# Gated attention and a top-2 expert layer: token rows scattered to expert slots in DRAM, in one engine block

## Time and profile before

| | |
|---|---|
| median of 3 runs | 1044.95 us (1043.86 to 1045.88) |
| profiled execution | 1039.82 us, its span 1038.1 us |
| busy share of the span | PE 96%, PE weight loads 82%, DVE 66%, ACT 46%, POOL 46% |
| mean granted TensorE clock | 0.988 |
| DMA | 63.42 MB, of which SP's queue 45.41 MB and POOL's queue 17.47 MB |

### The profile page before, as it was taken

One profiled execution on the slowest core, in us unless ns is written; L12 is line 12 of the kernel. 1 busy time (PEld: TensorE's weight loads), 2 busy tenths in 40 slices (PEclk: granted clock), 3 DMA queues, 4 the chain that ended last, 5 costly groups with the idle time before them and its releaser, 6 DMA issues. The chain is left out here.

```text
span 1038.1 us, 21103 instructions
## 1 busy us (share of the span) xinstructions
PE 993.9 (96%) x7314; PEld 855.4 (82%) x7314; DVE 682.9 (66%) x1607; ACT 477.9 (46%) x1502; POOL 482.6 (46%) x498
## 2 busy tenths in 40 slices
PE   6999999999999999999999997999999999999995
PEld 5778878878878778878878786799999899999995
DVE  5886895885885885885886866444455555444552
ACT  3664553553553553653553541344353544435351
POOL 7521071071071170270270153385858567585856
PEclk9999999999999999999999998999999999999998
DMA  9201110120020020021002001425345262523525
GB/s 247 84 9 54 42 48 13 40 61 7 34 61 20 20 61 33 8 61 56 4 0 61 3 1 41 133 37 132 61 107 127 62 147 35 132 56 102 122 55 66
DMA packets 49948, 63.42 MB, mean 61 GB/s; under 512 B 5976, under 2 KB 41714, under 8 KB 49906
## 3 DMA queue, kind: packets, MB, share of 16 engines
q1 hardware_dynamic: 37234, 45.41, 14.0%
q0 software_dynamic: 12672, 17.47, 10.0%
HBM read 46.45 MB, written 16.78 MB: 61 GB/s over the span
## 5 line engine op out<-in xcount | busy, mean ns | idle before, releaser
L1252 ACT ACTIVATE hid<-up,b 128x512 f32<-128x512 f32 x128 | 88.0, 687 | 86.2 <-PE up L1203 86.2
L722 ACT ACTIVATE work<-score,negmax 128x128 f32<-128x128 f32 x256 | 90.2, 379 | 80.6 <-DVE negmax L919 80.6
L1131 POOL DMA_INDIRECT out_dram<-eo,index_e x64 | 106.4, 1663 | 19.5 <-issue 18.9
L722 ACT ACTIVATE probs_odd<-score,negmax 128x128 f32<-128x128 f32 x256 | 90.2, 380 | 51.6 <-DVE negmax L919 51.6
L343 POOL TENSOR_SCALAR var<-mv 128x4 f32<-128x4 f32 (+1 forms) x17 | 3.8, 226 | 219.8 <-DVE mv L774 212.3
L1304 DVE TENSOR_TENSOR eo_raw<-down,b 128x256 f32<-128x256 f32 x64 | 25.9, 425 | 121.1 <-PE down L1217 121.1
L1297 DVE TENSOR_TENSOR hid_l<-hid,hid_h 128x512 fp32r<-128x512 f32 x128 | 88.7, 693 | 4.4
L675 ACT ACTIVATE q_sb<-proj 128x512 f32<-128x512 f32 x64 | 38.7, 604 | 108.9 <-PE proj L593 108.9
L1295 DVE CAST hid_h<-hid 128x512 fp32r<-128x512 f32 x128 | 54.7, 427 | 47.9 <-ACT hid L1252 46.2
L1260 ACT ACTIVATE eo<-eo_raw,gate_e 128x256 f32<-128x256 f32 x64 | 30.9, 506 | 118.1 <-DVE eo_raw L1304 118.1
L919 DVE TENSOR_REDUCE negmax<-score 128x4 f32<-128x512 f32 x128 | 81.9, 681 | 2.1 <-PE score L514 2.1
(11 more groups left out here) (217 smaller groups left out, 3067.2 us busy)
## 6 DMA issues: line engine op xcount, KB each, us to landing
w_raw<-fc1T_dram SPq DMA_DIRECT2D x9, 1024.0 KB, 5.3
w_raw<-fc_dram SPq DMA_DIRECT2D x9, 1024.0 KB, 9.3
rows<-x_dram SPq DMA_DIRECT2D x16, 512.0 KB, 4.6
out_dram<-rows SPq DMA_DIRECT2D x8, 512.0 KB, 3.0
xn_rows<-rows SPq DMA_DIRECT2D x8, 512.0 KB, 2.9
c_raw<-ctxT_dram SPq DMA_DIRECT2D x8, 256.0 KB, 3.9
c_raw<-ctxT_dram SPq DMA_DIRECT2D x16, 128.0 KB, 4.5
b<-fc2b_dram SPq DMA_DIRECT2D x9, 128.0 KB, 8.4
```

Source lines behind the costliest of these rows:

```text
L722: last = nc.scalar.activation(probs[j % 2][:, c, :], score[hh][:, b * P:(b + 1) * P], ACT.Exp, bias=negmax[:, j % 2, c:c + 1], accum_out=s ...
L1131: pool.indirect_dma_start(out=out_rows[:, :], out_offset=bass.IndirectOffsetOnAxis(ap=index_e[par][:, half * GB + i:half * GB + i + 1], ax ...
L1252: nc.scalar.activation(hid[m % 2][:, :], up[m % 2][:, :], ACT.Relu, bias=b1[par][:, m:m + 1]).then_inc(s_hid, 1)
```

## The change

1. Each group's rows are scattered to their slots. A tensor `disp` in DRAM has 8 x 1024 rows of 258 numbers: 256 features, the token number, and the exponential of the difference of the two best logits. A row stands in `packed` in SBUF; POOL issues eight indirect DMAs per group (two choices, four sequences), in `dispatch`, in the place where the one-hots were formed, so ahead of `copy_ck`. One-hots, T0/T1, the tables and their sums are gone, and so is the store of rows by SP. The second choices' real rank is compared with the capacity at once (`loc[:, 2]`).
2. `disp` is filled first by one SP DMA (zeros, and token number 4096, which is out of bounds), after the first two groups' loads.
3. Experts load their rows with plain SP DMAs, one per half, in place of gathers. DVE takes the token numbers and gate weights out of the last two columns (`meta`), at the start of each half.
4. Both parts stand in one block, and the block boundary is gone. In the hand-over the low parts of the first expert's weights go from POOL to DVE, one before the projection, one behind the slots; ACT's second high part moves behind the exponential; the warm-up matmuls of 3, 6 and 24 become one run of 40, and those of 26 ahead of the first transposes go.
5. The first two jobs of a group wait for the read-out of FA/FB (`s_f_split`) instead of the table sums.

The diff, cut to its core:

```diff
-MISC_PREV = {1: ["O0", "O1"], 2: ["XA", "XB"], 3: ["LG"], 4: ["PR"], 7: ["T0", "T1"]}
+MISC_PREV = {1: ["O0", "O1"], 2: ["XA", "XB"], 3: ["LG"], 4: ["PR"]}
...
         iteration(0, 1, False)
+        sp.wait_ge(s_blank, 1)
+        sp.dma_start(disp.rearrange("(t p) w -> p t w", p=P),
+                     blank[:, :].unsqueeze(1).to_broadcast([P, E * CAP // P, W])).then_inc(s_blank_out, 16)
...
+        def dispatch(g):
+
+            pool.wait_ge(s_disp_done, g)
+            pass_gate(pool, s_pool_gate)
+            me.mark(nc.gpsimd.tensor_scalar(token[:, :], token[:, :], float(TOK), None, ALU.add))
+            me.after()
+            pass_gate(pool, s_pool_gate)
+            copy(packed[:, :, D], token[:, :]).then_inc(s_packed, 1)
+            pool.wait_ge(s_gexp, g)
+            pool.wait_ge(s_slot_ready, g)
+            pool.wait_ge(s_packed, g)
+            pass_gate(pool, s_pool_gate)
+            for j in range(2):
+                for b in range(GB):
+                    pool.indirect_dma_start(
+                        out=disp[:, :], out_offset=bass.IndirectOffsetOnAxis(ap=slots[:, j, b:b + 1], axis=0),
+                        in_=packed[:, b, :], in_offset=None,
+                        bounds_check=E * CAP - 1, oob_is_err=False).then_inc(s_disp, 16)
+
+        def dispatched(g):
+
+            if isinstance(g, int) and g == 0:
+                pool.wait_ge(s_blank_out, 16)
+            else:
+                pool.wait_ge(s_disp, 16 * 2 * GB * g)
+            pool.sem_inc(s_disp_done, 1)
...
             if has_prev:
-                pool.wait_ge(s_slot_ready, g)
...
-                onehots(nc.gpsimd, 0).then_inc(s_onehot0, 1)
-                if has_next:
-                    onehots(nc.gpsimd, 1, (0, 1, 2)).then_inc(s_onehot1, 1)
...
+                dispatch(g)
             if has_next:
                 pool.wait_ge(s_k_ready, 8 * g + 8)
                 pool.wait_ge(s_cv_ready, g + 2)
                 copy_ck()
+            dispatched(g)
...
             add_bias(NG)
-            pool.wait_ge(s_e0_hi, 1)
-            nc.gpsimd.tensor_tensor(wq_l[:, :, :], w1_raw[:, :, :], wq_h[:, :, :].bitcast(f32), ALU.subtract).then_inc(s_e0_lo, 1)
             for half in range(2):
                 rstd(mv2, var2, rstd2, s_stats2, NG + half, s_rstd2, slice(2 * half, 2 * half + 2))
-            pool.wait_ge(s_e0_hi, 2)
-            nc.gpsimd.tensor_tensor(wo_l[:, :, :], w2_raw[:, :, :], wo_h[:, :, :].bitcast(f32), ALU.subtract).then_inc(s_e0_lo, 1)
...
+            dispatch(NG)
+            dispatched(NG)
...
-                pe.wait_ge(s_tb_done, 2 * g - 1 + n)
+                pe.wait_ge(s_f_split, 2 * g + 1 + n)
...
             misc("PR", av[0], NG)
-            wait_warm(24)
...
+            wait_warm(40)
...
-            dve.wait_ge(s_gexp, g)
-            n = me.mark(V.tensor_scalar(gden[:, :], gexp[:, :], 1.0, None, ALU.add))
-            me.after(n)
-            n = me.mark(V.reciprocal(gates[:, 0, :], gden[:, :]))
-            me.after(n)
-            me.mark(V.tensor_tensor(gates[:, 1, :], gexp[:, :], gates[:, 0, :], ALU.mult))
...
+            dve.wait_ge(s_disp_done, g)
+            V.tensor_tensor(slots[:, :, :], slot[:, :, :], late[:, :, :], ALU.add).then_inc(s_slot_ready, 1)
...
                     dve.wait_ge(s_rstd2, g)
+                    dve.wait_ge(s_disp_done, g)
                     normalise(xn2, x1, mv2, rstd2, s_xn2_ready)
...
+            dve.wait_ge(s_e0_hi, 1)
+            low(wq_l[:, :, :], w1_raw[:, :, :], wq_h[:, :, :]).then_inc(s_e0_lo, 1)
             residual_start(NG)
...
+            dve.wait_ge(s_e0_hi, 2)
+            low(wo_l[:, :, :], w2_raw[:, :, :], wo_h[:, :, :]).then_inc(s_e0_lo, 1)
...
+            for half in range(2):
+                n = 2 * e + half
+                sp.wait_ge(s_meta, n + 1)
+                load_rows(nxt, half)
+
+        def load_rows(e, half):
+            src = disp_v[bass.ds(e, 1), half * TOK:(half + 1) * TOK, :]
+            sp.dma_start(rows[half][:, :, :], src.rearrange("o (i p) w -> p (o i) w", p=P)).then_inc(rows_in[half], 16)
...
+        def meta(n, e, half):
+            dve.wait_ge(rows_in[half], 16 * (e + 1))
+            if not (isinstance(e, int) and e == 0):
+                dve.wait_ge(scatters[half], 16 * GB * e)
+                dve.wait_ge(s_eo_ready, GB * n - GB)
+            weight = rows[half][:, :, D + 1]
+            me.enter(3 * n)
+            V.tensor_copy(index[half][:, :], rows[half][:, :, D])
+            i = me.mark(V.tensor_scalar(den[:, :], weight, 1.0, None, ALU.add))
...
+            i = me.mark(V.reciprocal(den[:, :], den[:, :]))
+            me.after(i)
+            V.scalar_tensor_tensor(out=gate[half][:, :], in0=share[:, :], scalar=tanh_g[:, 1:2], in1=den[:, :],
+                                   op0=ALU.mult, op1=ALU.mult).then_inc(s_meta, 1)
```

More of the change, by code:

```diff
@@ L856, in route_slots @@
             me.after(n)
[L857 removed]
+            n = me.mark(V.tensor_tensor(loc[:, 2, :], loc[:, 2, :], loc[:, 1, :], ALU.add))
             n = me.mark(V.tensor_tensor(slot[:, 0, :], slot[:, 0, :], loc[:, 0, :], ALU.add))
@@ L1042, in experts @@
     b2 = [sb(f"b2_{n}", [P, D]) for n in range(2)]
-    rows = [sb(f"rows_{n}", [P, GB, D]) for n in range(2)]
+    eo = [sb(f"eo_{n}", [P, GB, D]) for n in range(2)]
     rT_h, rT_l = sb("rT_h", [P, DK, TOK], f32r), sb("rT_l", [P, DK, TOK], f32r)
@@ L1085, in step @@
         def step(e, nxt, par, first=False):
-            if not first:
+            if first:
+                sp.wait_ge(s_e0_lo, 2)
+            else:
                 sp.wait_ge(s_w_lo, e)
-            for half in range(2):
-                sp.wait_ge(gathers[half], 16 * GB * (e + 1))
             load_expert(sp, fc1T, fc2, nxt, w1_raw, w2_raw, s_w_in)
@@ L1111, in _ @@
     def _(pool):
-        def columns(e, par):
-            nc.gpsimd.tensor_copy(index_e[par][:, :], index[:, bass.ds(e * EH, EH)]).then_inc(s_index_e, 1)
-        def gather(columns_, half):
-            pass_gate(pool, s_pool_gate)
-            for i in range(GB):
-                pool.indirect_dma_start(
-                    out=rows[half][:, i, :], out_offset=None, in_=xn2_dram[:, :],
-                    in_offset=bass.IndirectOffsetOnAxis(ap=columns_[:, half * GB + i:half * GB + i + 1], axis=0),
-                    bounds_check=N + PAD - 1, oob_is_err=False).then_inc(gathers[half], 16)
         def scatter(n, e, par, half):
@@ L1172, in _ @@
                 step(EB * t + i, i)
-        for half in range(2):
-            pool.wait_ge(gathers[half], 16 * GB * (E + 1))
         for done in scatters:
@@ L1180, in _, with transpose_rows @@
         mm = nc.tensor.matmul
-        def transpose_rows(gathered, half):
-            pe.wait_ge(gathers[half], gathered)
+        def transpose_rows(loads, half):
+            pe.wait_ge(rows_in[half], loads)
             for k in range(DK):
@@ L1196, in group @@
                     pe.wait_ge(s_rt_split, 2 * n + 2)
-                    if not (isinstance(e, int) and e == 0):
+                    if isinstance(e, int) and e == 0:
+                        pe.wait_ge(s_e0_lo, 2)
+                    else:
                         pe.wait_ge(s_w_lo, e)
@@ L1291, in group @@
                 dve.wait_ge(biases[par], 16 * (e - par) + 32)
-                V.tensor_copy(gate_e[par][:, :], gate[:, bass.ds(e * EH, EH)])
+            meta(n, e, half)
             for m in range(HK):
```

259 lines of the change are left out of this document (84 added, 175 removed).

## The result

The changed kernel takes 1071.66 us (median of 4 runs, 1067.97 to 1075.79), the kernel before 1044.5 (4 runs, 1043.86 to 1045.88): a ratio of 1.0262, 95% interval 1.0239 to 1.0284. It is slower, where 1028.4 and faster were predicted. Its profiled execution took 1067.97 us (span 1066.2, mean granted clock 0.966).

The account below looks back on a forecast made before the run. PE, busy 96% of the span, was taken as the bound. Terms -13.2 - 0.5 - 1.2 - 0.7 + 0.7 (slow clock) - 1.7 = -16.6 us gave 1023.2 profiled, 1028.4 median; forecast's own range 1020 to 1036, overall 1017 to 1050.

Parts of the forecast that it names:

- T0 and T1 at the six turns: Turns between attention groups: table jobs go, so the next Q starts earlier; 2.2 us a turn, 13.2 us gained.
- three signs of being wrong: A K that waits for `ck`, dispatch spacing above 1.74 us, or a load of x held by the fill.
- Rival A: POOL between slots and `ck`: scatters spaced 1.85 us make the keys late; +6.3 us, 1051; chance 0.19.
- Rival A2: Dispatch in attention: each scatter also waits 0.64 us for a DVE operation, spacing 1.99; +14 us, 1059; chance 0.05.
- Group 0: After group 0, PE's 0.5 us wait for DVE's release of the table banks goes.
- Group 7: Table jobs and DVE's twelve one-hots go, so the last scores' maximum starts sooner; 1.2 us gained, at worst 0.
- Hand-over: Attention to experts: 4.4 us won before slots goes to scatters and DRAM; rows land 0.7 us sooner (-3 to +6).
- Experts at nothing: Expert stage: PE's order unchanged; DVE's five added operations per half, about 0.85 us, hidden in idle time; no cost.
- Tail: Last scatter no longer stands behind eight gathers in POOL's queue, starting at 1028.04 instead of 1029.79: -1.7 us.
- Fill of `disp`: 8.45 MB in SP's ring, ahead of the x load due at 75.91; cost 0 unless slow.
- rival C: The fill of `disp` takes 74 us and holds an x load, +10 us: -6.6 in all, 1038; chance 0.08.
- B: Hand-over: rows land as late as the slowest scatter, 8.5 us not 3.4; +5.1, so -11.5, 1033.4; chance 0.11.

Follow-up runs that it names:

- pairs and 1088 B: Changed kernel with each group's eight scatters in four pairs, other work between, and rows padded to 1088 B: 1023.61 us, ratio 0.9806 to before.
- pairs of 1032 B: Changed kernel with each group's eight scatters in four pairs, other work between, row width unchanged: 1026.72 us over five runs, ratio 0.983 to before.

## Why the prediction was wrong, point by point

- **The step that failed** is the first, "T0 and T1 at the six turns". It priced the eight scatters on POOL's own queue alone, and asked only whether `ck` would be late for K. What came late was the increment that tells ACT of PE's own Q (6.4 us late in the turn shown). In place of -2.2 a turn stands +4.4 on average ((481.6 - 455.3)/6). None of the three signs of being wrong that the prediction names came up: no K waits for `ck`, the spacing is 1.28, and the fill holds no load of x. The group that ends with the turn shown is 5.6 us longer than the same one with pairs and 1088 B. The parts add up to 5.7: 5.3 more between the last K matmul and V, 1.0 more from V to FA (the slow clock), and 0.6 less from FA to the next Q.
- **The gain at the turn is there once the hold is gone**: 75.9 to 73.96 a group with pairs of 1032 B, -1.9 for all eight scatters. With half of them, spaced by 2.15, it is 73.72, -2.2. Predicted -2.2 for eight.
- **The scatter's price was right**: 1.28 us spacing, predicted 1.35 (and a hair below the 1.29 that stood as the least). Rival A had the mechanism right for its own price, as the accumulating dispatch shows: at 1.85 it is the keys that PE waits for. The price was wrong.
- **Rival A2 is real, but hardly met in the turns.** The prediction weighed it by the Trainium skill, "SBUF — State Buffer", "SBUF: two separate sides", by which some operations of DVE keep GpSimd from writing DMA descriptors until they end. The trace agrees where DVE runs an operation with both inputs in SBUF. In the hand-over the first scatter starts beside DVE's subtract of weights, takes 2.43 us in place of 0.97, and ends 0.97 after the subtract does (666.62 + 2.29 = 668.91). In group 1 two scatters beside such an operation take 1.67 and 1.28. In the 14 profiles with plain scatters in the dispatch, 91 start with 0.2 us or more of such an operation left, and all end 0.84 to 1.11 us after it does. Beside operations that read PSUM nearly nothing is added: 0.97 at 462.38, where DVE forms `negmax`, and 0.97 beside `xT_l` (run with the dispatch behind the copies), from which A2 took its 0.64. So A2 cost 1.5 us once and little in the turns. The sign of the result was that of A and A2, the mechanism neither's.
- **Group 0** gained 1.0, predicted 0.5; the first Q of group 1 lies between 76.9 and 78.3 over the runs, so the one trace does not tell these apart. **Group 7** lost 4.6 by the hold; with pairs it is unchanged (78.1 against 78.0) where -1.2 was predicted, with half the scatters -0.9.
- **Hand-over**: -2.9, predicted -0.7. The normalise is at 0.74 as predicted. Slots come 25.1 us after the projection's start against 30.6, so 5.5 sooner where I had 4.4; from there to the rows it takes 17.7 us against 15.1, predicted 18.8. The terms: the first scatter at +0.9, 10.4 to the last, 2.7 to SP's issue, 3.7 for the load. In the lines below, the first scatter of this row takes 2.43, since it waits for DVE's subtract (`w_split`), and the load takes less than the earlier trace rows. The prediction put that subtract behind the slots and did not ask what it would do to the scatters:

```profile
650.77 0.74 DVE L757 TENSOR_SCALAR packed<-rows,mv,rstd 128x256 f32<-128x256 f32 x2 [1.27 <-POOL rstd L328]
...
666.40 0.17 DVE L839 TENSOR_TENSOR slots<-slot,late 128x8 uint32<-128x8 f32 x1
...
666.62 2.29 DVE L738 TENSOR_TENSOR w_split<-w_raw,w_split 128x2048 fp32r<-128x2048 f32 x1
```

```profile
667.45 2.43 POOL L399 DMA_INDIRECT disp<-packed,slots  x1 [10.54 <-DVE slots L839]
670.19 0.97 POOL L399 DMA_INDIRECT disp<-packed,slots  x1 [0.30 <-issue]
...
677.87 0.97 POOL L399 DMA_INDIRECT disp<-packed,slots  x1 [0.30 <-issue]
```

```profile
680.61 0.92 SPq L1052 DMA_DIRECT2D rows<-disp  x2
```

```profile
684.31 1.97 PE L1119 MATMUL rT<-ident,rows 128*128 128x128 f32 x8 [9.10 <-DMA rows<-disp]
```

- **Experts at nothing** was wrong by 3.2 us: the halves from the first `up` to that of the last take 344.8 us against 341.6. It is not `meta`, which stays, while with rows of 1088 B and pairs they take 342.0. The loss comes in stretches: the `down` matmuls of one half start 118 ns apart in place of 113, the `up` matmuls of the next 233 in place of 229, and then a stretch at full pace follows; the granted clock is 1.00 in both. In the changed kernel this begins with the sixth half, and halves two to five take 22.76 as before. In all 13 profiles with rows of 1032 B it goes on to the end, in the two with 1088 B only the first such stretch is there. So it goes with the width, but the width alone does not start it; the cause was not settled.
- **Tail**: from the start of the last `up` matmul to the end of the last scatter 16.35 us against 17.74, -1.4, predicted -1.7. The last scatter follows its `eo` by 1.2, not 0.3, since it stands behind the other three at 1.86 each. What follows that scatter is 1.1 us shorter as well.
- **Fill of `disp`**: nothing, as predicted. It took 37.1 us to land and the next x load was issued at 75.01, against the earlier trace rows; rival C falls. So does B: the rows landed sooner than in the forecast.

With pairs and 1088 B, 1023.6 is below the 1028.4 that the prediction had for the median. Between the profiles the gain is 16.2 us (1038.1 to 1021.9), against the sum of 16.6. That close a match is in part luck: the six turns gave 10.8 of the 13.2 and group 7 none of its 1.2, while the hand-over gave 2.4 for 0.7. The reasons for a gain held, and the loss came from a wait that the prediction did not ask about.

## What to carry to other kernels

A DMA that POOL issues can cost more than its place in POOL's queue: in a tight row it can delay what other engines learn from PE, so try other work between such DMAs, two at a time or one every 2 us, and measure again. Look also at what DVE runs when such a DMA starts: beside an operation with both inputs in SBUF it waited for the end of that operation here. When a wait in the profile has no releaser ("remote", on one core), look when the semaphore rose and not when its maker ended. A new tile of an odd width moves all tiles behind it; if a stage gets slower whose code has not changed, try another width.

## What the runs showed of the hardware that was not expected

- In attention, eight plain scatters at 1.28 us from start to start hold PE's semaphore increments for up to 7.3 us (7.1 to 8.8 over the other runs with such rows), four for 3.0, three for 1.6, two for 0.4 at most. Of four at 2.15 us none is late by 0.25. DVE's and ACT's, as far as the traces hold them, are not held.
- In group 1 of the changed kernel increments are late only from about the seventh scatter on (by up to 3.6 us); in later groups from the third. Its row is not even: the first and the fourth scatter wait for DVE, so the second starts 1.97 us after the first and the fifth 1.58 after the fourth. Counted from the fifth, the seventh is again the third of a tight row. That is a reading of one row and was not tried; the second to fourth, at 1.29 and 1.28, held nothing.
- Open: why rows of four plain scatters, as tight, hold nothing in the expert stage; and by which path POOL's work reaches PE's increments.
- A scatter that accumulates takes 1.55 to 1.6 us and one that writes 0.97, the first of a row 1.1.
- A scatter that starts beside an operation of DVE with both inputs in SBUF waits for its end: 2.43 us in the hand-over, 1.2 to 1.7 in attention. An operation that reads PSUM does not do that (0.97).
